# GpSimd's copy of the doubled query rows, one unit earlier, in a two-layer attention kernel on one core

## The reference

```python
scores = jnp.einsum('bhqd,bhkd->bhqk', q, k) / scale
c2p_att = jnp.einsum('bhqd,hpd->bhqp', q, pos_k)
c2p = jnp.take_along_axis(c2p_att, c2p_pos, axis=-1)
p2c_att = jnp.einsum('bhkd,hpd->bhkp', k, pos_k)
p2c = jnp.swapaxes(jnp.take_along_axis(p2c_att, p2c_pos, axis=-1), -1, -2)
scores = scores + (c2p + p2c) / scale
probs = jax.nn.softmax(scores, axis=-1)
ctx = jnp.einsum('bhqk,bhkd->bhqd', probs, v)
```

## Time and profile before

| | |
|---|---|
| median of 3 runs | 2524.29 us (2523.96 to 2525.17) |
| profiled execution, own time | 2521.2 us |
| its span, first to last instruction | 2519.6 us |
| attention stage, about | 157 us to 1205 us of the span |
| GpSimd copies of query rows (L814) | 32, of 1881 ns each |

### The profile page before, as it was taken

How to read it: one execution, slowest core, us unless ns; L and a number is a source line. 1 busy time by engine, 2 the same in 40 slices (tenths; PEclk the granted TensorE clock), 3 DMA queues, 4 the chain that set the end, 5 groups by cost and what they waited for, 6 DMA issues and landing times. The chain is left out here.

```text
span 2519.6 us, 47313 instructions
## 1 busy us (share of the span) xinstructions
PE 1898.4 (75%) x13556; PEld 1405.2 (56%) x13557; DVE 1630.6 (65%) x3986; ACT 992.0 (39%) x2034; POOL 1124.7 (45%) x1470
## 2 busy tenths in 40 slices
PE   6868888888888888888599997756235279999752
PEld 3426666766766666767366764434225158876421
DVE  8946777776777676777755551687757954444434
ACT  3435666665656565665133232422011023332000
POOL 4134555455555555563121210377540045554665
PEclk9978999998999998999799998877665579999876
DMA  4679999999999999999312100000001534447333
GB/s 154 217 247 321 318 333 321 314 328 300 340 306 328 300 341 298 339 333 294 112 53 67 67 0 1 1 0 1 0 22 48 200 107 155 153 148 124 109 110 107
DMA packets 296213, 460.85 MB, mean 183 GB/s; under 512 B 38380, under 2 KB 229596, under 8 KB 296028
## 3 DMA queue, kind: packets, MB, share of 16 engines
q1 hardware_dynamic: 267548, 392.06, 48.6%
q0 software_dynamic: 28480, 66.39, 10.6%
HBM read 236.91 MB, written 221.38 MB: 182 GB/s over the span
## 5 line engine op out<-in xcount | busy, mean ns | idle before, releaser
L980 DVE CUSTOM_DVE_ANT_0 c2p<-bank,c2p 128x512 f32<-128x512 f32 x512 | 351.2, 686 | 189.2 <-PE bank L876 177.2
L989 DVE COPY probsT<-bank 128x512 f32<-128x512 f32 x512 | 351.2, 686 | 70.2 <-PE bank L886 69.9
L938 ACT ACTIVATE c2p<-c2p,neg_max 128x512 f32<-128x512 f32 x512 | 371.7, 726 | 12.4 <-DVE neg_max L980 12.3
L953 ACT COPY a_stage<-bank 128x320 f32<-128x320 f32 (+1 forms) x512 | 211.4, 413 | 366.6 <-PE bank L845 347.8
L886 PE MATMUL bank<-ident,c2p 128*128 128x128 f32 x2048 | 330.1, 286 | 3.3 <-ACT c2p L938 2.9
L2177 POOL DMA_INDIRECT p_x_tile<-y_d,p_token x160 | 152.5, 953 | 285.6 <-POOLq L1878 162.2
L886 PEld LDWEIGHTS bank<-ident,c2p 128*128 128x128 f32 x2048 | 267.3, 148 | 14.4 <-issue 6.1
L876 PE MATMUL bank<-ident,p2c 128*128 128x128 f32 x1280 | 235.3, 283 | 0.0
L857 PE MATMUL bank<-tab,k 96*128 96x320 bf16 (+1 forms) x512 | 164.4, 321 | 73.1 <-DVE b_stage L932 54.7
L845 PE MATMUL bank<-tab,q 96*128 96x320 bf16 (+1 forms) x512 | 160.5, 313 | 68.2 <-POOL q L814 47.2
L871 PE MATMUL bank<-k,q 96*128 96x384 bf16 (+1 forms) x512 | 160.1, 313 | 34.9 <-issue 33.3
(11 more groups left out here) (271 smaller groups left out, 3904.8 us busy)
## 6 DMA issues: line engine op xcount, KB each, us to landing
p2c_d<-b_stage SPq DMA_DIRECT2D x64, 640.0 KB
c2p_d<-a_stage SPq DMA_DIRECT2D x64, 640.0 KB, 6.9
p2c_d<-b_stage SPq DMA_DIRECT2D x64, 576.0 KB
c2p_d<-a_stage SPq DMA_DIRECT2D x64, 576.0 KB, 7.2
p2c<-p2c_d SPq DMA_DIRECT2D x256, 144.0 KB, 5.9
c2p<-c2p_d SPq DMA_DIRECT2D x256, 144.0 KB
o_sorted_d<-p_o_pair SPq DMA_DIRECT2D x80, 256.0 KB
p_w_all<-in_experts SPq DMA_DIRECT2D x4, 3072.0 KB, 21.6
```

The source lines that it names most:

```text
L938: act.activation(c2p[:, w % 4, j, :], c2p[:, w % 4, j, :], ACT.Exp, bias=neg_max[:, w % 2, j:j + 1], scale=-1.0).then_inc(exp_done, 1)
L953: act.copy(staged(a_stage, wa % 2, wa % TPB)[:, j, :], bank[A_BANK][:, 0:width(wa % TPB)]).then_inc(a_copied, 1)
L980: dve.tensor_tensor_reduce(c2p[:, w % 4, j, :], bank[S_BANKS[(HB * w + j) % 3]][:], c2p[:, w % 4, j, :], -SCALE, LOWEST, ALU.add, ALU.min, ...
L989: dve.tensor_copy(probsT[:, wp % 2, j], bank[T_BANKS[j % 2]][:].rearrange("p (k q) -> p k q", k=TPB)).then_inc(probsT_copied, 1)
```

## The change

The copy for a group moves from the end of GpSimd's step with t = 3 to the end of its step with t = 2, behind the end columns of table B of that step. The first group's copy is issued before the first step, behind one memset. The number of copies, their size and the loads that feed them are the same.

```diff
@@ -806,18 +806,24 @@
-                        if w % TPB == TPB - 1 and is_unit(*ahead(i, w, TPB + 1)):
+                        if w % TPB == 2 and is_unit(*ahead(i, w, TPB + 2)) and (is_unit(i, w) or w > BODY - TPB):
                             g = w // TPB
                             wait_count(pool, q_top_loaded[(g + 2) % 4], Q_LOADS * (i + (2 if g == 3 else 1)))
                             pool.wait_ge(b_ends_copied, BODY * ib + wb + 1)
                             apart(pool)
-                            pool.tensor_copy(q6[TWICE:2 * TWICE, (g + 2) % 4], q6[0:TWICE, (g + 2) % 4]).then_inc(q_doubled, 1)
+                            double_q((g + 2) % 4)
                             pool.wait_ge(q_doubled, 4 * i + g + 3)
                             apart(pool)
...
+                    def double_q(slot):
+                        pool.tensor_copy(q6[TWICE:2 * TWICE, slot], q6[0:TWICE, slot]).then_inc(q_doubled, 1)
+
                     pool.memset(v_h[:, :, TILES * (D + 1):], 0.0).then_inc(pad_set, 1)
+                    pool.wait_ge(pad_set, 1)
+                    double_q(0)
+                    pool.wait_ge(q_doubled, 1)
                     each_step(pool, step)
```

## The result

| | before | changed |
|---|---|---|
| median | 2524.73 us (4 runs, 2523.96 to 2527.54) | 2500.84 us (4 runs, 2493.55 to 2502.30) |
| ratio | | 0.9895, 95% interval 0.9879 to 0.9911 |
| profiled execution, span | 2519.6 us | 2498.8 us |

The change gives 23.9 us (1.05%). The direction was forecast rightly. The forecast was 2512 us, a gain of 12.2 us or 0.48%, with a range of 2491 to 2524 us. The time lies in the range; the gain is about twice the one forecast.

The account below looks back on a forecast made before the run. The stage was taken as paced by its DMA transfers, PE's stall lying beside them. From 2521.2 us, 2.7 (start), 7.5 (jumps) and 2.0 (first body) came off, giving 2509.0; plus 3.1 to the median, 2512.1 us, range 2491 to 2524.

Parts of the forecast that it names:

- The stall would go and mostly not pay: In groups, PE's 2.35 us stall before table A vanishes; waits for staged tables replace it; groups stay near 30 to 31 us.
- The full 99 us: Stall and lower clock at 3.8 us in 26 groups, all refunded if nothing else waited; 2423 us by the skill's rule.
- The start, 2.7 us: At the stage's start PE waits 2.89 us for the first copy; issuing it earlier brings back 2.7 us.
- The jumps, 7.5 us: Behind the loop's five jumps DMA idles 2.4 us each; a larger backlog uses 1.5 of it, 7.5 us in all.
- The steady state, 0 us: In groups between others, transfers take 30.0 to 31.0 us anyway, gain 0 to 0.9 us, taken as 0.
- the first body, 2 us: In the loop's first body, slack yields 2 us once.
- the forecast's own upper bound: Start's 2.7 us plus at most 14 us: 2.4 us at each of five jumps and 2 us of first-body slack.
- The copy in the step with t = 3: Fills there begin about 1.95 us later and reads follow; queued transfers cover it, cost 0; uncovered, up to 55 us.
- The rival "slower": Late fill in the step with t = 3 starves the DMA engines; over 2529 us, chance 0.09.
- Nothing but the start: Slack is already used up and jumps idle for their own cause; only 2.7 us remain, 2519 to 2524 us, chance 0.20.
- Transfers give way: In groups, transfers speed up once the stall is gone; 2421 to 2490 us, chance 0.13.

Follow-up runs that it names:

- relief_before: Kernel before, writes and skewed reads of both staged tables cut to two of four batches from unit 16 on: 2490.41 us (0.9870).
- relief_after: Changed kernel, writes and skewed reads of both staged tables cut to two of four batches from unit 16 on: 2407.66 us (0.9533).
- copy_no_wait: Changed kernel plus a same-size copy into a spare tile at the old place on GpSimd's queue, nobody else waiting: 2532.92 us (1.0038).
- between: Changed kernel with the copy moved into the step with t = 3, behind its fills and ahead of its end columns: 2501.71 us (0.9905).
- between_late: Copy between fills and end columns of the step with t = 3, plus a spare copy at the old place without a waiter: 2524.26 us (1.0007).
- between_again: Changed kernel with the copy between fills and end columns of the step with t = 3, measured once more: 2499.43 us (0.9901).
- start_alone: Kernel before with only the first copy early, all others at the old place: 2522.44 us (0.9992).
- between_stall: Copy between fills and end columns of the step with t = 3; PE's group-first table A also waits for c2p's fill: 2510.24 us (0.9945).
- changed_third: The changed kernel measured a third time, unaltered: 2506.01 us (0.9932).
- groups_alone: Changed kernel without the early first copy, which stays behind the first end columns; copies in groups moved: 2509.92 us (0.9932).

## Why the prediction was right and wrong

*The stall would go and mostly not pay.* Right. The 63.5 us of waits for the copy are gone, PEclk in the group is 1.00, and the group shown stays at 30.9 us; the waits stand at a_stage and b_stage, as forecast. The runs relief_before and relief_after show it: 83 us where transfers have room, 24 where they have not. The full 99 us, and with them 2423 us, did not come. That was the time by the rule of the Trainium skill that I set against my step (page "Perfetto Trace Analysis", section Identifying the Most-Contended Engine, which calls the occupancy of 16 DMA engines misleading). It was no empty warning: at the same share of 1.04 the rate was 319 (copy_no_wait) to 332 GB/s (between), so the share shows that transfers bind and not how fast they can go.

*The start, 2.7 us.* 2.4 us in the trace. Right.

*The jumps, 7.5 us.* 8.8 us in the jump steps and the groups behind them, 5.9 and 7.6 in the two other traces. Right in size. That idle DMA time shrank there is shown in part only: added up in steps of 1 us from 200 to 1130 us, the share that is missing to 1 is 13.2 us before and 8.7, 10.5 and 7.1 in the three traces of the changed kernel, 3 to 6 us less.

*The steady state, 0 us, and the first body, 2 us.* Here the gain was missed: 11.8 us instead of 0 (9.2 and 10.6 in the two other traces) and 7.4 instead of 2 (3.7 and 5.8). The step that failed is "I take 0 in the steady state". It rested on a rate held at 328 to 339 GB/s in the groups, and it left the sentence "In return the next step's fills and reads, and its loads of k, are 2 us earlier" without a price: I looked at the cover of the step that the copy moved into and not at the one that it left. The runs showed in its place that a copy of 1.88 us in the step with t = 0 costs 27 us by itself (between_late against between_again, known to 8), by packets that take 3% longer at the same share; and that taking this lateness away while PE still stalls gives 12 us (start_alone to between_stall), about what was missed. PE's stall of 2.35 us, by far the more visible wait in the profile, costs 11 us by itself, and nothing where the copy is late as well. That the time lies in the range is in part luck: it is beyond the forecast's own upper bound, a gain of 16.7 us, and inside only by the 16 us that were added for the rival in which transfers give way.

*The copy in the step with t = 3.* Priced at 0. changed_third stands 0.0031 above between_again, its neighbour on the same chip; the two other ratios of the changed kernel, from other chips, don't. Within 0.003 it is nothing, which leaves the term as it was. The rival "slower", by starved DMA engines there, did not come: the share of the window stays 1.06.

*The rivals.* "Nothing but the start" is refuted by groups_alone, 0.9932. "Transfers give way" had a grain of truth: the rate did rise, by 9 of the 18 GB/s to the 339 that I had set as its end.

What stays open is how lateness on GpSimd slows the stage when its DMA engines are hardly idle (17.8 us of 930 in between_late, 13.9 in between_again). The packets of GpSimd's loads and of the skewed reads take longer, those of the writes hardly; whether that is from reads bunching with GpSimd's loads or from something else was not tried, and neither was which of the late instructions counts, the fills, the loads of k or the end columns. The split of the 24 us is also only as good as the intervals: 27 us for the late copy and 11 us for the stall, each to about 8 us, and they do not add.

## What to carry to other kernels

When a blocking instruction is moved, price both of its places for every instruction behind it on its own queue, and not only the wait of the engine that is seen to stall; a queue with more work in one step than the step is long is the first to look at. A long wait beside saturated transfers may be worth far less than it shows: here 11 us, known to 8, of the 99 that the lengths of the steps showed. Cutting the bytes evenly over all partitions was the experiment that told; a cut to half of the partitions was not, since the packets that were left took longer. A share of DMA above 1 was a right sign here that transfers bind, but 3% more came through at the same share.

## What the runs showed of the hardware

With writes cut from 128 to 64 partitions a packet of 5120 bytes took 310 ns on the average, against 204 ns, so that a quarter fewer bytes left the DMA share at 0.99 instead of 1.04. And at an equal share of 1.04 the rate was 319 to 332 GB/s, though the kernels move the same data: a packet took 81.1 to 82.4 ns on the average where GpSimd's copy was not late in the step with t = 0, and 83.6 to 84.4 ns where it was. Most of the difference is in GpSimd's own loads (103 to 109 ns against 116 to 125 ns) and in the skewed reads.
